# Eleven more product tiles for the first expert steps of a two-layer kernel, and a new order of work

## The chip, the core and the metric

The kernel runs on one core of a Trainium2 chip. A core has five engines with a queue of instructions each: TensorE (PE in the profile) multiplies matrices and writes to eight PSUM banks, VectorE (DVE), ScalarE (ACT) and GpSimd (POOL) do elementwise work, and SyncE (SP) issues the DMA transfers. Each engine takes its own instructions strictly in order; semaphores order the engines against one another. The metric is the device time of one execution in microseconds.

## What is computed

Two transformer-like layers on x of shape (4, 512, 128), all in float32. Cut to what matters:

```python
xn = layernorm(x)
x = x + linear_attention(xn) + mixture(xn)      # layer 1
#   mixture: 64 experts of width 88 and a shared one; 8 experts per token by a grouped top-k
#   rw = route(xn)                               # (tokens, 64), eight non-zero per token
#   out = shared(xn) + sum_e rw[:, e] * ((silu(xn @ Wg[e].T) * (xn @ Wu[e].T)) @ Wd[e].T)
xn = layernorm(x)
x = x + window_attention(xn) + bitlinear_ffn(xn) # layer 2
#   window attention: 8 heads of 16, for each token the 32 nearest of the last 64 by a learned distance
```

## The kernel before

**Expert steps.** The routed and shared experts are stacked and cut into 46 slabs of 128 hidden units (`NF`), the same for each of the four batch rows, so there are 184 expert steps n. In a step TensorE makes the gate part in a bank G and the up part in a bank U, each as three matmuls of 512 columns (high weights by high input, high by low, low by high), ScalarE writes silu(G) into a product tile, VectorE multiplies the tile by U (`products`), and for the 44 routed slabs of each row the tile is multiplied by the spread routing weights `Rb[k]`: even steps on VectorE (`weights`), odd ones on GpSimd (`tiles`). TensorE then adds `WdT @ tile` to bank A (`downs`); a float32 matmul shows as two records. Before a step, ScalarE makes the high part of the weights (`Whi`) and GpSimd or VectorE the low part (`Wlo`).

**The ring.** The product tiles are five, `S[n % RING]`. `silus` therefore waits, before step n writes its tile, until the down matmul of step n-5 is done. With two banks G and two banks U, TensorE itself can run two steps beyond the last tile.

**Where routing weights come from.** Row 0's routing is a long row of small VectorE instructions (letters y): normalise, gate, grouped top-8, weights; then TensorE turns them (`MATMUL bank_X<-cst,xn`, the fourth y of its queue), ScalarE and VectorE make `RW`, and four small matmuls (`bank_X<-RW,sel`, letter s) with a ScalarE copy each give `Rb[0]` to `Rb[3]`. Slabs 0 and 1 need no routing; slab 2 does. So no more than two down matmuls can run before `Rb[0]` exists.

**Other work.** Linear attention of row b (letters a: the matmuls q0, q1, k0, k1, then qn = `bank_X<-cst,PR`, kn = `bank_X<-PR,cst`, sim = `bank_X<-GWk,wqk`, r0, r1 = `bank_X<-wout,z`, m, att) is a chain over four engines: between kn and r0 lie a VectorE clamp, ScalarE logarithm and exponential, four GpSimd passes over `PR` and `z`, and a softmax that goes to and fro. The setup of layer 2's weights (u) is a chain of VectorE instructions with four TensorE steps, wf and wp among them. Layer 2 of row b (h head, d distances, k top-32 by MAX8 and MATCH_REPLACE8 on VectorE, g and t gather, f feed-forward) starts when bank A of the row has been copied to `mo`.

**Order.** The order on each engine is written out by hand as a string of letters in `ORDER` (lines 37 to 72); `weave` takes the next step of the part that each letter names. A letter e on TensorE is half an expert step (G or U), so 368 stand there; m is one down matmul. On ScalarE x is `Whi`, e is silu; on GpSimd l is `Wlo`, m a weighted tile. ScalarE has two function tables to load in turn, one for silu and gelu and one for logarithm and exponential; a load is issued wherever neighbours in the string need different ones (`logarithms`, L1264, and the automatic one, L1259).

Of the kernel before, what the change touches and what calls it, by code (L numbers as in the profile page):

```python
# [15 lines left out]
NF = 46  # L16
# [28 lines left out]
        "eeeeemmeeeehheemmmeeemymmeeemeemahheeemeaehemadedadmeeeadeedatdateemmmeemeeedtemetmdemeameemteeateat"
        "eeaemmestemstfeemfemfetetftemmefmmetfteeeeemfeeeefmsmeemmmeeeetmmtetseeteeeeatmeehmmeemmmteaeeeeeeeh"
        "mhmmeeehhmhmheeehmeeemeeemeemameeehmeeededmdeaedaeemmaetdaeemmdtmeeemeeeeememeeetdatdmeematmteeeamma"
        "teeeetftemeeeemmemfeeetmtemeteemeememeeteftmeeemmteteemmtmtmfhftffthfhhfhhhhfffhfdddfdfdtfttdtddtttt"
# [5 lines left out]
        "gemkaeklemaygyeyemkkyykegleemkkfkgekmkeklekmfgeemeelfgefgemgeemhhhhlyhheyyyyyeyyyyymeehylyyyeyyyeymm"
        "yyeemlheemyeelmhaehhheaoemoolemookkkkkkakokaekoakkgoeemkeakklekamkgkaeemkklemekgemkkakkagkleemkkkgek"
        "fekmgekkkfemkgkkelkefkekkmleefmgemeemglegeeemlgaehhhhemhhgaeemleemhehhelmeemeemlehhheoomeolemooekkkk"
        "akkekoakmkakkeklekgmaooeekamkeelmakkkekgemkegkkkakkaelgmeemkekkklgemefkemgekkkelmkkeegemkkgkeelmgkke"
        "megfhhhhgfhhgfhhhfhhfhooookkfkkokkkkkkkookokkkkggfkkkgkkkkkgkgkkkkkgkgkkgkkkkkkkkggggg",
    "act":
        "xyxxyyxeexcxeecxxeexxexayasxsseeysaexxxeeaexxeeaxauxexeeuxxeuxexeeyxexyexexexexexeexxeexexexexexxeex"  # L60
        "xxeexeexxeyexxsexexeyxmexeesexxxssxexehxeexexyeyhexxexhhxexehxexehxheeehxkekxyenxknknnkaxnxankkngeka"
        "nngexxeenxeaxexexeexxnegxaengaxeexxexexgssyefeexxgxexexeefxexxfegexxfexgsxesmyexexeyhxehxhxeeehxexxe"
# [4 lines left out]
        "lllyyllllllmammaaaamlalalmalmllmlmllmylmyllmmlllmlmllmymlllmlmllmlmllmlmllmlllmllmlmyyllhmolmllmylhm"
        "holmooomoqoaopaqaaalalqllamplpmllmaqlmmlpqlppmqllmlmlmpllqplpmqllmmlplplpymlylmlholmlmllymlmllmmlhlh"
        "olooolaqloooaammalapqalmqampallpmlqlmlpmlqlppmqmlplqmllmqlmplpmllmpllplpmllmlmlholmmllmlmhllholomoom"
        "loaqoaaaalmlopalmllaqmaqllmplpmqqpllmlmlppmqllmllqpmmlppmqmppphohhoooooqoqoqpppqqpppqppqpqpp",  # L70
# [1660 lines left out]
```

## Time and profile before

| | |
|---|---|
| three runs | 785.96, 787.54, 788.20 us; median 787.54 |
| profiled execution | 788.22 us, its span 786.4 us |
| busy, share of the span | PE 90%, DVE 81%, POOL 57%, ACT 53% |
| granted TensorE clock, mean | 0.932 of full |
| chain that ended last | PE 44%, DVE 35%, POOL 7%, ACT 5%, issue 5%, DMA 4% |

The span is the profiled execution from its first to its last instruction; 1.8 us of the execution's own time lie outside it. Busy shares are means over stages that differ: TensorE is nearly full from 16 us to 690 us, VectorE nearly full in some stretches and not in others, and after the last expert step the work is a chain. The chain of waits is followed back from the last instruction, so its shares say who held the end up.

### The profile page before, as it was taken

What the parts mean: (1) busy time and instruction counts of PE and PEld (TensorE: products, weight loads), DVE (VectorE), ACT (ScalarE), POOL (GpSimd) and SP (SyncE); (2) the same over time, 40 slices, a digit from 0 to 9 for tenths busy, and PEclk for the clock granted to TensorE, in tenths of its full rate; (3) what the DMA queues carried; (4) which work ended last, traced back from release to release, by engine and by line L of the source; (5) the groups of instructions that cost most, each with busy time, mean ns of one, the idle gap of its engine ahead of it and who ended that gap; (6) DMA issues with size and microseconds to landing.
All of it is one profiled execution on the core that took longest, in us unless ns stands there. A gap on an engine that the chain in (4) does not pass through costs nothing.

```text
span 786.4 us, 11674 instructions
## 1 busy us (share of the span) xinstructions
PE 704.6 (90%) x3368; PEld 500.7 (64%) x3368; DVE 640.7 (81%) x2562; ACT 419.7 (53%) x757; POOL 451.9 (57%) x535
## 2 busy tenths in 40 slices
PE   3998999999999889999998999999998999978733
PEld 2645666666576666776676677666675776768623
DVE  3877787768999999849799999765799899659974
ACT  3754444566675555455675774456683754465300
POOL 2265366546676864854567856654668768433441
PEclk9979999999997999999998999999999999996555
DMA  9920000000000000000000000001000000010000
GB/s 287 358 68 1 1 0 0 2 1 16 17 1 10 9 15 11 9 15 20 13 1 8 11 12 16 8 7 26 14 2 9 10 15 15 19 31 8 18 23 17
DMA packets 25695, 22.14 MB, mean 28 GB/s; under 512 B 1892, under 2 KB 23424, under 8 KB 25120
## 3 DMA queue, kind: packets, MB, share of 16 engines
q1 hardware_dynamic: 25632, 21.40, 9.1%
q8 instruction: 27, 0.44, 0.2%
q14 instruction: 36, 0.29, 0.1%
HBM read 19.17 MB, written 2.23 MB: 27 GB/s over the span
## 4 chain that ended last, share of the span: by engine, by line
PE 44%; DVE 35%; POOL 7%; ACT 5%; issue 5%; DMA 4%; SPq 0%; DVEq 0%; POOLq 0%; ACTq 0%
PE bank_A L505 11%; PE bank_X L505 11%; PE bank_U L505 10%; PE bank_G L505 9%; DVE Wk L1193 8%; DVE S L790 6%; DVE m L1190 6%; DMA vw<-vscratch 4%; DVE GWk L790 2%; DVE sm L794 1%; POOL wT L1501 1%; POOL Wlo L1501 1%; ACT Ed L1259 1%; DVE wT L790 1%; ACT L1264 1%
## 5 line engine op out<-in xcount | busy, mean ns | idle before, releaser
L505 PE MATMUL bank_A<-S,WdT 128*128 128x512 f32 x368 | 186.8, 612 | 5.9 <-POOL S L1501 4.4
L1501 POOL TENSOR_TENSOR Wlo<-Wgu,Whi 128x256 fp32r<-128x256 f32 x138 | 108.3, 789 | 108.8 <-ACT Whi L1259 108.4
L790 DVE TENSOR_TENSOR S<-S,bank_U 128x512 f32<-128x512 f32 x184 | 123.7, 678 | 56.9 <-PE bank_U L505 36.0
L1259 ACT ACTIVATE S<-bank_G 128x512 f32<-128x512 f32 x184 | 108.2, 594 | 106.7 <-PE bank_G L505 98.0
L1501 POOL TENSOR_TENSOR S<-S,Rb 128x512 f32<-128x512 f32 x88 | 117.8, 1340 | 63.3 <-DVE S L790 59.3
L1259 ACT ACTIVATE Whi<-Wgu 128x256 fp32r<-128x256 f32 x184 | 74.0, 413 | 78.7 <-PE bank_U L505 69.8
L505 PE MATMUL bank_G<-xH,Whi 128*128 128x512 f32 x184 | 96.9, 526 | 5.5 <-POOL Wlo L1501 2.8
L505 PEld LDWEIGHTS bank_A<-S,WdT 128*128 128x128 f32 x368 | 66.7, 193 | 49.9 <-issue 29.2
L505 PE MATMUL bank_U<-xH,Whi 128*128 128x512 f32 x184 | 91.7, 498 | 5.0 <-DVE S L790 4.6
L790 DVE TENSOR_TENSOR S<-S,Rb 128x512 f32<-128x512 f32 x88 | 83.4, 951 | 2.4 <-ACT Rb L1259 0.5
L1193 DVE MATCH_REPLACE8 Wk<-m,Wk 128x79 f32<-128x79 f32 x384 | 81.8, 223 | 0.0
L505 PE MATMUL bank_G<-xL,Whi 128*128 128x512 f32 x184 | 73.5, 400 | 0.0
L505 PE MATMUL bank_U<-xH,Wlo 128*128 128x512 f32 x184 | 73.3, 399 | 0.0
L505 PE MATMUL bank_G<-xH,Wlo 128*128 128x512 f32 x184 | 73.3, 399 | 0.0
L505 PE MATMUL bank_U<-xL,Whi 128*128 128x512 f32 x184 | 73.3, 398 | 0.0
L1501 POOL TENSOR_TENSOR wT<-wT 128x256 f32<-128x256 f32 (+1 forms) x62 | 41.4, 667 | 42.9 <-DVE wT L790 40.5
L1190 DVE MAX8 m<-Wk 128x8 f32<-128x79 f32 x384 | 63.2, 225 | 0.0
L505 PEld LDWEIGHTS bank_G<-xH,Whi 128*128 128x128 f32 x184 | 35.2, 191 | 28.4 <-issue 23.2
L505 PEld LDWEIGHTS bank_U<-xH,Whi 128*128 128x128 f32 x184 | 35.1, 191 | 27.3 <-DVE S L790 12.7
L1259 ACT ACT_TABLE_LOAD x35 | 44.9, 1283 | 1.5 <-PEq L1721 0.7
L505 PEld LDWEIGHTS bank_G<-xL,Whi 128*128 128x128 f32 x184 | 35.4, 193 | 15.5 <-issue 11.4
L505 PEld LDWEIGHTS bank_U<-xL,Whi 128*128 128x128 f32 x184 | 35.2, 191 | 12.6 <-issue 8.1
(233 smaller groups left out, 1440.9 us busy)
## 6 DMA issues: line engine op xcount, KB each, us to landing
vw<-vscratch SPq DMA_DIRECT2D x32, 158.0 KB
Wgu<-in_Wgu SPq DMA_DIRECT2D x2, 2048.0 KB, 15.3
xs<-in_x SPq DMA_DIRECT2D x4, 256.0 KB, 7.0
wqk<-in_w_qkv SPq DMA_DIRECT2D x1, 1024.0 KB, 7.3
Wgu<-in_Wgu SPq DMA_DIRECT2D x1, 1024.0 KB, 9.6
vscratch<-mo SPq DMA_DIRECT2D x4, 256.0 KB
out<-xs SPq DMA_DIRECT2D x3, 256.0 KB, 2.3
Wgu<-in_Wgu SPq DMA_DIRECT2D x1, 512.0 KB, 5.1
```

Of the source, the lines that this page charges most:

```text
L505: return engine.matmul(dst, lhsT, rhs, start=start, stop=stop)
L790: return engine.tensor_tensor(dst, a, b, op)
L794: return engine.tensor_scalar(dst, a, s1, None, op0)
L1190: top[i] = own(engine.max(w8[:, i, 8 * r:8 * r + 8], v[:, i, :]))
L1193: p = engine.match_replace(wk[:, i, :], w8[:, i, 8 * r:8 * r + 8], v[:, i, :], TAKEN)
L1259: return engine.activation(dst, src, f, bias=bias, scale=scale, accum_out=acc)
L1264: engine.preload_act_table_set(LNEXP)
L1501: return engine.tensor_tensor(dst, a, b, op)
```

## The change

Eleven tiles of layer 2, which nothing writes until layer 2 of row 0 begins, take the products of steps 0 to 10. Steps 11 on go round the five tiles `S` as before, shifted. So the first step that must wait for a down matmul is step 16 (for that of step 11), where it was step 5. The helper `early_tile` takes 512 columns of a tile. With that, all five strings of `ORDER` are other strings; no instruction with data is added or taken away, but there are 74 table loads in ScalarE's program where there were 64.

```diff
@@ ORDER, the start of the string of TensorE and of ScalarE; the other strings differ in the same way
-        "yyeeyeeeeemaeeeaemaeeeeeeyaesasmsmsmaeeaeeeemmmmmmeeemeeamueamaueeeeuemmeeeaumeeeeyeeemmyeeemymmmeem"
+        "yyeeyyeeemeemeeeaeeaeeaeeeeeeeeeeeaeyaeseesmammsasmmmmmuemmmeemauaeeeeaemmueammumeeeeyeeymeeeeeemy"
-        "xyxxyyxeexcxeecxxeexxexayasxsseeysaexxxeeaexxeeaxauxexeeuxxeuxexeeyxexyexexexexexeexxeexexexexexxeex"
+        "yxxxyyexexexecexxceexxeexexexxeaeaxxyexsesxyassaeexaaxexeuxexuuxeeyxxeeeyexxxexexxeeexxeexxexexyexey"
...
+        early = [mo, yT, ksq, hf, hg, wT[0], wT[1], kp, mk2, Ed[0], Ed[1]]
+
+        def early_tile(t):
+            return (t[:, :, :].rearrange("p a w -> p (a w)") if len(t.shape) == 3 else t)[:, 0:T]
+
+        tiles_of = [early_tile(t) for t in early] + [t[:, :] for t in S]
+
+        def product_tile(n):
+
+            return tiles_of[n] if n < len(tiles_of) else S[(n - len(early)) % RING][:, :]
+
+        def tile_free(n):
+
+            return n - RING + 1 if n >= len(tiles_of) else 0
...
-                    if n >= RING:
-                        sc_.wait_ge("down", n - RING + 1)
-                    emptied(act(S[n % RING][:, :], t[:, :], ACT.Silu), "g", n)
+                    if tile_free(n):
+                        sc_.wait_ge("down", tile_free(n))
+                    emptied(act(product_tile(n), t[:, :], ACT.Silu), "g", n)
...
-                    mm(T_["A"][:, :], WdT[:, m % NF, :], S[m % RING][:, :], m % NF == 0, m % NF == NF - 1).then_inc(
+                    mm(T_["A"][:, :], WdT[:, m % NF, :], product_tile(m), m % NF == 0, m % NF == NF - 1).then_inc(
```

`products`, `weights` and `tiles` take `product_tile(n)` in the same way.

**TensorE around the turned routing weights of row 0** (`bank_X<-cst,xn` from L514, which is L529 in the changed file). Before:

```order
58 L505 MATMUL bank_G<-xL,Whi 128x512
59 L505 MATMUL bank_G<-xH,Wlo 128x512
60 L514 MATMUL bank_X<-cst,xn 128x128 x4
61 L505 MATMUL bank_X<-wqk,Gs 128x512
62 L505 MATMUL bank_U<-xH,Whi 128x512
63 L505 MATMUL bank_U<-xL,Whi 128x512
64 L505 MATMUL bank_U<-xH,Wlo 128x512
65 L505 MATMUL bank_X<-RW,sel 128x512
66 L505 MATMUL bank_X<-cst,PR 128x1 x8
67 L505 MATMUL bank_X<-RW,sel 128x512
68 L505 MATMUL bank_A<-S,WdT 128x512
69 L505 MATMUL bank_X<-RW,sel 128x512
```

The changed kernel at the same place:

```order
87 L520 MATMUL bank_X<-wqk,Gs 128x512
88 L520 MATMUL bank_G<-xH,Whi 128x512
89 L520 MATMUL bank_G<-xL,Whi 128x512
90 L520 MATMUL bank_G<-xH,Wlo 128x512
91 L529 MATMUL bank_X<-cst,xn 128x128 x4
92 L520 MATMUL bank_X<-cst,PR 128x1 x8
93 L520 MATMUL bank_U<-xH,Whi 128x512
94 L520 MATMUL bank_U<-xL,Whi 128x512
95 L520 MATMUL bank_U<-xH,Wlo 128x512
```

The turn stood behind 17 half expert steps and two down matmuls; it now stands behind 27 half steps and the same two down matmuls.

**GpSimd from the same place to the end of the key norms of row 0** (`PR`, `z`: the attention chain; `<-...,Rb`: weighted products). Before:

```order
10 L1501 TENSOR_TENSOR Wlo<-Wgu,Whi 128x256 x6
11 L1501 TENSOR_TENSOR S<-S,Rb 128x512
12 L1501 TENSOR_TENSOR PR<-GWk,wqk 128x1024
13 L1501 TENSOR_TENSOR S<-S,Rb 128x512 x2
14 L1501 TENSOR_TENSOR PR<-PR 128x512
15 L1501 TENSOR_TENSOR PR<-PR,z 128x512
16 L1562 TENSOR_SCALAR PR<-PR 128x512
17 L1501 TENSOR_TENSOR z<-PR 128x512
```

The changed kernel:

```order
10 L1516 TENSOR_TENSOR Wlo<-Wgu,Whi 128x256 x9
11 L1516 TENSOR_TENSOR PR<-GWk,wqk 128x1024
12 L1516 TENSOR_TENSOR Wlo<-Wgu,Whi 128x256
13 L1516 TENSOR_TENSOR hf<-hf,Rb 128x512
14 L1516 TENSOR_TENSOR Wlo<-Wgu,Whi 128x256
15 L1516 TENSOR_TENSOR wT<-wT,Rb 128x512
16 L1516 TENSOR_TENSOR kp<-kp,Rb 128x512
17 L1516 TENSOR_TENSOR Ed<-Ed,Rb 128x512
18 L1516 TENSOR_TENSOR S<-S,Rb 128x512
19 L1516 TENSOR_TENSOR PR<-PR 128x512
20 L1516 TENSOR_TENSOR PR<-PR,z 128x512
21 L1577 TENSOR_SCALAR PR<-PR 128x512
```

Between the wide `PR<-GWk,wqk` and the first `PR<-PR` stood two weighted products; five weighted products and two `Wlo` stand there now.

**ScalarE at the head of layer 2 for row 2**, expert steps 150 to 153. In the kernel before:

```order
457 L1259 ACT_TABLE_LOAD
458 L1259 ACTIVATE hb<-bank_X,b 64x1
459 L1259 ACTIVATE Whi<-Wgu 128x256
460 L1259 ACT_TABLE_LOAD
461 L1259 ACTIVATE S<-bank_G 128x512
```

In the changed kernel, where the attention of row 3 (`rq`, `PR`, `z`) stands among it:

```order
459 L1279 ACT_TABLE_LOAD
460 L1274 ACTIVATE rq<-rq 128x8 x2
461 L1274 ACTIVATE PR<-z 128x512
462 L1274 ACTIVATE PR<-PR 128x512
463 L1274 ACT_TABLE_LOAD
464 L1274 ACTIVATE S<-bank_G 128x512
465 L1274 ACTIVATE Whi<-Wgu 128x256
466 L1274 ACTIVATE mo<-bank_X 128x512
467 L1274 ACT_TABLE_LOAD
468 L1274 ACTIVATE hb<-bank_X,b 64x1
469 L1279 ACT_TABLE_LOAD
470 L1274 ACTIVATE z<-z 128x512
```

The attention of row 3 came between expert steps 158 and 168 of VectorE's string; it comes between 145 and 163 now.

## Rows read from the trace of the kernel before

**Rows 1.** Busy time by stretch: us, then busy us (instructions) of each engine, PEclk.

```profile
16.29:36.40 20.11, 19.98 (x69) 13.94 (x69) 18.04 (x62) 13.48 (x22) 5.38 (x10) 1.00 1.04 367
36.40:63.70 27.30, 25.24 (x102) 12.33 (x102) 19.19 (x43) 12.52 (x24) 17.15 (x14) 0.81 0.30 79
...
480.00:560.00 80.00, 78.98 (x321) 52.62 (x321) 57.01 (x175) 41.24 (x79) 42.30 (x54) 1.00 0.06 15
560.00:690.00 130.00, 121.22 (x675) 89.65 (x674) 114.41 (x527) 74.07 (x130) 89.75 (x103) 0.99 0.04 12
```

**Rows 2.** Timeline of TensorE, 35 to 64 us: start, us, instruction, releaser.

```profile
35.51 0.40 PE L505 MATMUL bank_G<-xH,Whi 128*128 128x512 f32 x1
...
37.37 0.66 PE L514 MATMUL bank_X<-cst,xn 128*128 128x128 f32 x4 [0.99 <-DVE xn L795]
...
39.51 0.50 PE L505 MATMUL bank_X<-RW,sel 32*128 32x512 f32 x1
39.94 2.01 PE L505 MATMUL bank_X<-cst,PR 128*128 128x1 f32 x16
```

**Rows 3.** Timeline of TensorE, 82 to 93 us, at full clock.

```profile
82.31 0.39 PE L505 MATMUL bank_G<-xH,Whi 128*128 128x512 f32 x1
...
83.00 0.40 PE L505 MATMUL bank_U<-xH,Whi 128*128 128x512 f32 x1
...
92.97 0.40 PE L505 MATMUL bank_G<-xH,Whi 128*128 128x512 f32 x1
```

**Rows 4.** The chain of waits, three pieces: start, us, what.

```profile
7.98 1.28 ACT L1264
...
343.63 1.72 PE bank_A L505 x4
...
608.93 1.28 ACT L1264
```

**Rows 5.** Timeline of VectorE: `RW`, weighted products, attention of row 3.

```profile
38.69 0.75 DVE L798 SCALAR_TENSOR_TENSOR RW<-RW,cst,bank_X 128x512 fp32r<-128x512 f32 x1 [0.79 <-ACT RW L1259]
40.68 5.11 DVE L790 TENSOR_TENSOR S<-S,Rb 128x512 f32<-128x512 f32 x3 [0.45 <-ACT Rb L1259]
62.39 0.68 DVE L790 TENSOR_TENSOR S<-S,Rb 128x512 f32<-128x512 f32 x1
...
586.13 0.68 DVE L794 TENSOR_SCALAR z<-bank_X 128x512 f32<-128x512 f32 x1
...
611.07 0.67 DVE L1038 TENSOR_REDUCE rq<-z 128x8 f32<-128x512 f32 x1
```

**Rows 6.** Timeline of GpSimd, row 0's attention chain and its neighbours.

```profile
42.45 2.79 POOL L1501 TENSOR_TENSOR PR<-GWk,wqk 128x1024 f32<-128x1024 f32 x1
...
54.17 1.20 POOL L1501 TENSOR_TENSOR PR<-PR 128x512 f32<-128x512 f32 x1 [4.36 <-ACT PR L1259]
...
60.01 0.74 POOL L1501 TENSOR_TENSOR Wlo<-Wgu,Whi 128x256 fp32r<-128x256 f32 x1
```

**Rows 7.** Timeline of TensorE, where the first r of the attention starts.

```profile
68.77 1.09 PE L505 MATMUL bank_X<-wout,z 64*64 64x128 f32 x16
```

**Rows 8.** Costliest groups: line engine op, count | busy us, mean ns | idle before.

```profile
L1501 POOL TENSOR_TENSOR S<-S,Rb 128x512 f32<-128x512 f32 x88 | 117.8, 1340 | 63.3 <-DVE S L790 59.3
L1193 DVE MATCH_REPLACE8 Wk<-m,Wk 128x79 f32<-128x79 f32 x384 | 81.8, 223 | 0.0
L1190 DVE MAX8 m<-Wk 128x8 f32<-128x79 f32 x384 | 63.2, 225 | 0.0
```

**Rows 9.** Timeline of ScalarE, 7 to 10 us.

```profile
7.55 0.42 ACT L1259 ACTIVATE Whi<-Wgu 128x256 fp32r<-128x256 f32 x1 [5.54 <-DMA WdT<-in_WdT]
7.98 1.28 ACT L1264 ACT_TABLE_LOAD   x1
9.28 0.45 ACT L1259 ACTIVATE lnv<-lnv 128x8 f32<-128x8 f32 x2
```

**Rows 10.** Who waited for whom, 0 to 100 us: one row of ScalarE's tile waits.

```profile
ACT S L1259 <- PE bank_A L505: 2.0, 3, 1.0
```

More of the change, by code:

```diff
@@ L45 @@
[L45 to L48, printed above, removed]
+        "yyeeyeeemeemeeeaeeaeeaeeeeeeeeeeeeaeyaeseesmammsasmmmmmuemmmeemauaeeeeaememmueammumeeeeyeeymeeeeeemy"
@@ new lines @@
+        "mmeeeemeeemeeeemmmeeemmeeemeyeeemmeemeeesmmseeseemsmeeeeememememememeeeeeymeyemmyheeeeeeemmmemeeeeee"
+        "heehhmmeheeeemmmeehehmemmeheemeymeeeemhmemeeedeeadeemedeadmdamemateetademeeaeeeaemmmdteemeeetmdmemee"
+        "emmatetmaeeaeteeemetatemesmeesememfeetetmfteeemmfteetmemfeetfeeemmeethmtfmfteeeeefeetseeesemmeymmeet"
+        "ymmmyheehhemeehhemhehmeeemeememeeeeemmeheeymeeeaeeeaeeadadadmadadememmtmmtdemeememeetdeeeemmaetemaed"
+        "eaemtetmaeeeesmmeemmteestefeeftemmeeetmefteeefetefemmfteetemfmmmefeeesetmeseetatatheteememamaeeeaeeh"
@@ L54 @@
[L54 to L58, printed above, removed]
@@ new lines @@
+        "ylyyeyeyeyyyyylemeyyymeyyymeyyeyymleeyeymyyemyyelemeemleemeelmeeeemlyyhehehehmyylyhyyeeyyheyyyymyeyy"
+        "lmhyeemyyyyeemelmhehheemhemylehooemeoemlaoeokkakkkkkkkokkaeeoeglkekaokakmmemekakkkeamkleeamgegkkklem"
+        "ekakgemekkaekgklmyeemykegekkfkklgemkkkgkeyfekmelkyygeemhhfghheeelmfemgelemeghyhyyyyyyyyyemhyeyyhyyyh"
+        "yelmyeemyhyeelymehemheoeylemaemoaooaokakakolekokkkkkaemegaemokkkelkemakkkeekkekgmkelmagkeakkeemklekg"
+        "mekkekgmefkklgemekkeefmkkgkfkegmkkkklefeelemgeagaemhghehhhhemlaeemaghaaeahaemhleehmehhelmoeoemooeemk"
@@ new lines @@
+        "klokkkkkkekookkgemoekkkemlkegeakkmkelkgkemekkemeklkakeegmemekkgeklmekkemgeklekmgkfkeemkeklemkegkemke"
+        "kgghfhhhgfhhgfhhhhfhhfooofkkkokkkkokkookkkfkogkgkkkkkkkkgkgkgkkkkkkkkkkkggkgkkkkkggggg",
+    "act":
+        "yxxxyyexexexecexxceexxeexexexxeaeaxxyexsesxyassaeexaaxexeuxexuuxeeyxxeeeyexxxexexxeeexxeexxexexyexey"
+        "xeesxxsesxexexexexexexxeesxyemxyexeexxxheexxeexhxehhexxheeexxexhexexhexeyhxekxkxeeknxkennkxnennkkaxe"
+        "gnaexkxexeaxnexnegxexenaxeexnagxaexneexxegxesexxsefexgxexegfexxeyxeemxfxgegfexexxexsxseexeyehyxhxhhe"
+        "xhexxeexheexxxeheexhxekkyxeexxxankaknnnxkaeknnkenegxekeanxxxeneexxgeanxaexneneexgxxsexesefgxxexexefe"
+        "gxxexfexgexfexxexsemseegxgxxeahaexexhxehaexhhaexxeehehxxexhexkeknexknxenxxakknexanenngxkkenkneegxxxe"
+        "neexxexennexxgexxeexegxfeexexxexgexxeexefgxxeeeegmgfhfhhhhfhhfhkfnnkknnnnkknnknnfgnnkkgnngnnggggg",
@@ L66 @@
     "pool":
[L67 to L70, printed above, removed]
+        "lllyylllllllllalmlmmmmaaaaaamalmmlllmylylmmllmllmmllmlymlllmmlllmmllmllmlyyllmmllllmlmholmlymlmlhlml"
@@ L71 @@
+        "homllomolmolooqlamolpmlaqqaaallamlaqmappmlllmqpmllplpmlqmllpqmpplmlqllpmlmllpplmyymllholmllmhlmymllh"
+        "olllooaoaammaaqmoolalmapqolmlaqlmllmpqpmllmlqpmllpplqmmllmlqplppqmllmlpllmpplamlhoaaaaamalalmhmllhol"
+        "molomllolqoomqopmllqmplplmqlmlmllqmlpmlpplmqllmlplmqlmpmpmqppphohhooooqooqopqppqpqppqqpppqpp",
 }
@@ L814, in products @@
                 for n in range(total):
-                    s = S[n % RING]
+                    s = product_tile(n)
                     yield
```

26 lines of the change are left out of this document (9 added, 17 removed).

## The prediction

> **What bounds the kernel now.** I read first the busy time by stretch [rows 1]; its columns after the length are PE, weight loads, DVE, ACT, POOL, the granted clock, DMA share and GB/s. From 16.29 to 36.40 us TensorE is busy 19.98 of 20.11 us and VectorE 18.04: both are near full, since row 0's routing and the first expert steps go on together. From 36.40 to 63.70 TensorE looks busy (25.24 of 27.30) but at a mean clock of 0.81. Later VectorE alternates: 57.0 of 80 us from 480 to 560, where row 2's experts are finished, and 114.4 of 130 from 560 to 690, where the top-k work of layer 2 lies beside the experts.
>
> The timeline of TensorE then shows what "busy" hides [rows 2]. Half step 16 starts at 35.51. The turn of the routing weights waits 0.99 us for VectorE and starts at 37.37. The spread that follows takes 0.43 us to its successor (39.51 to 39.94), and then comes qn, sixteen records of one column, 2.0 us; behind it the clock drops to 1.2 GHz until about 52 us. TensorE has nothing better to do there: with five tiles, and only steps 0 and 1 free of routing, it stands at most two steps beyond tile 6. The wait itself is hardly visible: ScalarE waited for a tile 2.0 us in three pieces [rows 10], because the old order never let it come to a longer one.
>
> How much is lost, by counting. A half expert step takes 0.69 us at full clock (82.31 to 83.00, [rows 3]), a down matmul 0.86 (1.72 for two, [rows 4]). From half step 16 at 35.51 to half step 40 at 92.97 are 57.5 us. In them stand 24 half steps (16.6 us), 15 downs (12.9 us), and other work of about 16.9 us at full clock, an estimate from the timeline: turn 0.5, four spreads 1.7, k1 0.9, qn 1.9, kn 1.1, sim 1.15, r0 and r1 2.2 ([rows 7] has one), m 1.95, att 1.05, the layer 2 setup 4.45. That is 46.4, so 11.1 us of the stretch are lost to low clock and to waiting.
>
> **The change part by part.** *Start.* ScalarE's string now begins with the logarithm of the lengths instead of `Whi`. Before, `Whi` waited for a transfer until 7.55 and the table load began at 7.98 [rows 9]; the lengths are ready at about 7.2, so the routing chain, and with it TensorE's first expert step, comes 0.7 us earlier.
>
> *Filling the hole.* Ten more half steps stand ahead of the turn. They cost TensorE 6.9 us there, and VectorE six more products and a `Wlo`, some 4.5 us in its full stretch; so `RW`, which is made at 38.69 now [rows 5], comes later. From 34.8 (35.51 less 0.7) eleven half steps and k1 bring TensorE to the turn at 43.3. VectorE is ready for it by then (its 4.5 us more on 37.4, less 0.7, is 41.2), so nobody waits there, and after it TensorE has steps for which no routing is wanted. If it never waits until half step 40, it gains the 11.1 us and the 0.7: 11.8.
>
> *What is late next.* The chain of linear attention. In GpSimd's queue five weighted products and two `Wlo` now stand between the wide `PR` product and the first `PR<-PR`. Turn at 43.3 plus 0.5, qn 1.9, wide product 2.79 [rows 6], two `Wlo` at 0.74 [rows 6], five weighted products at 1.34 [rows 8]: GpSimd comes to the chain at 56.7, not at 54.17. From there to r0 it took 14.6 us (54.17 to 68.77, [rows 6, 7]), of which one weighted product and one `Wlo` (2.1 us) no longer stand in between: r0 at 69.2. TensorE has before r0, counted from 34.8, 17 half steps (11.7), 12 downs (10.3), k1, qn, kn and sim (5.0), spreads, turn and the first setup step (2.5): it is there at 64.3 and waits 4.9 us, with the setup's wf, r1 and four half steps queued behind. So of 11.8 the front keeps 6.9. Bounds: 11.8 if the wait is hidden; about 0 if GpSimd's five products are as slow as beside VectorE's and the clock drops behind qn as it does now (three downs at 2.0 instead of 0.86 and their neighbours, 5 us).
>
> The row on that: VectorE took 5.11 us for three weighted products while GpSimd worked, and 0.68 for one alone [rows 5]. The Trainium skill, "GPSIMD Engine Reference", section 1, Specifications, says that GpSimd shares its SBUF interfaces with VectorE and contends with VectorE instructions that have two SBUF inputs; by that rule, and this trace agrees, bunching eleven weighted products on both engines speaks against the change. With a stretched duration in place of the mean, r0 and the total would come some 2 us later.
>
> *Ten more table loads.* There are 64 pieces of 1.28 us now, and on the chain that ended last stand ten of them, the first at 7.98, the last at 608.93 [rows 4]. If the ten new ones lie on the chain as often, 10 x 10/64 x 1.28 = 2.0 us. Bounds: 0 and 12.8. The activation behind a load starts at 9.28, 0.02 us after its end [rows 9]. The Trainium skill, "ScalarE: Activation LUTs", section What ACT_TABLE_LOAD costs, gives 1.28 us for the load and 1.38 for a drain, 2.66 together; the load agrees, the drain is not seen here. By the page this term would be 4.2 us.
>
> *Attention of row 3.* It moves from VectorE's steps 158 to 168 to its steps 145 to 163, out of the full stretch and partly into the one with slack [rows 1]. Its four passes of 512 columns on VectorE at 0.68 ([rows 5]: first at 586.13, last at 611.07) are 2.7 us, with the small ones about 5.4. I take 2.7 as gained; bounds 0 and 5.4. What pays is the head of layer 2 for row 2, among which it now stands, in part by the table loads above.
>
> *Tail.* Behind the last expert step the strings are the same but for one more round of top-k and one more turn. A round is four MAX8 and four MATCH_REPLACE8 at 0.22 [rows 8], 1.8 us; it stands where VectorE also waits for `mo`, so I take half, 0.9 (bounds 0 and 1.8).
>
> *Between.* From 93 to 690 us all strings differ, but the milestones stand within a few steps of their old places relative to the experts, and all work is the same. Its stalls I take as unchanged, with 5 us to either side.
>
> Sum: -6.9 + 2.0 - 2.7 + 0.9 = -6.7 us. On the profiled execution's 788.2 that is 781.5; the median is 0.7 below that execution, so 780.8.
>
> **The rivals.** *More of it is kept.* If the wait for r0 is hidden and the attention of row 3 gives its full 5.4: -11.8 - 5.4 + 2.0 + 0.9 = -14.3, 773. For it: the chain up to 84 us runs over the setup's VectorE steps, which are also earlier now. Against it: GpSimd's queue, counted above.
>
> *The gain in front is given back.* Stretched products and a clock that falls behind qn leave about nothing in front; table loads and row 3's attention cancel: 788. For it: the clock fell behind qn in this very place. Against it: half steps follow qn now, not a spread and a tile that isn't ready, and no idle time stands ahead of it.
>
> *Table loads at the head of row 2.* Seven of the ten new loads are in expert steps 150 to 169 (17 instead of 10), between `ln`, `hb`, `met` and the distances, which feed the top-k that fills VectorE afterwards. If all ten are on the path, 12.8 instead of 2.0: -6.9 - 2.7 + 0.9 + 12.8 = +4.1, 791.6. It turns to slower from about seven loads on the path (8.7/1.28). For it: ten loads are on the chain now, several of them at such heads. Against it: at 480 to 560 us VectorE has 23 us to spare.
>
> *The tiles do nothing.* If the old order had lost its time not to the ring but to VectorE's routing chain alone, more tiles would only add work ahead of it. Against it: the loss is after 37.4, when the routing is done. This ends like the second rival and shares its chance.
>
> **How the numbers follow.** Forecast, 776 to 785: 0.46. More kept, under 776: 0.19. Given back, 785 to 790: 0.18. Slower by table loads or by another stall of the new order: 0.17. A measurement here tells 0.3% (2.4 us) from no change. So faster 0.65, same 0.18, slower 0.17. The range 771 to 791 leaves 0.05 below and 0.14 above; the forecast's own is 776 to 785.
>
> **What would show it.** Right: in the new timeline TensorE reaches the turn at 42 to 45 us without a wait; the clock between 36 and 64 us stays near 1; half step 40 with 20 downs done stands at about 88 to 90 us (before, with three downs less, 92.97); r0 starts at 68 to 71 with several us of idle before it, and GpSimd's z or PR ahead of it in the chain; 74 table loads. `mo` of row 3 is copied 5 to 8 us earlier than now. Wrong: a clock of 0.5 behind qn again; an idle TensorE between 43 and 60; a top-k of row 2 that starts no earlier than before.

## The result, and the profile after

| | before | after |
|---|---|---|
| median of the runs | 787.87 us (4) | 806.62 us (4; 803.84 to 808.82) |
| span of the profiled execution | 786.4 us | 806.6 us |
| granted TensorE clock, mean | 0.932 | 0.925 |

The ratio is 1.0238, its 95% interval [1.0196, 1.028]: the changed kernel is 18.8 us slower, where 6.7 us faster was forecast. It lies above the range too. That it is slower is clear; whether by more than 2% isn't, since the interval begins at 1.0196.

The stretches of [rows 1] in the changed kernel, and one more, in the same columns:

```profile
16.29:36.40 20.11, 20.08 (x74) 14.84 (x75) 17.11 (x57) 14.26 (x23) 5.03 (x9) 1.00 1.04 367
36.40:63.70 27.30, 22.81 (x107) 13.00 (x106) 25.12 (x49) 12.89 (x27) 18.15 (x16) 0.89 0.30 80
400.00:440.00 40.00, 36.39 (x197) 25.61 (x196) 28.77 (x85) 26.04 (x45) 23.70 (x26) 0.87 0.01 2
480.00:560.00 80.00, 78.73 (x399) 54.87 (x397) 65.19 (x277) 42.21 (x81) 52.96 (x66) 1.00 0.05 13
560.00:690.00 130.00, 121.07 (x587) 85.61 (x587) 116.31 (x513) 78.85 (x133) 83.86 (x94) 0.99 0.05 13
```

From 36.4 to 63.7 us VectorE (the third number pair) went from 19.2 to 25.1 us of busy time, and TensorE was busy for 22.8 us instead of 25.2. Right behind it, from 64 to 93 us, TensorE is as busy as before, but at a granted clock of 0.87 (the third number from the end) where the kernel before had 1.00; the changed kernel stands first:

```profile
64.00:93.00 29.00, 27.38 (x122) 18.08 (x121) 23.47 (x42) 8.15 (x14) 10.94 (x10) 0.87 0.00 1
64.00:93.00 29.00, 27.30 (x142) 18.52 (x141) 22.18 (x46) 12.14 (x22) 11.15 (x11) 1.00 0.00 1
```

From 400 to 440 VectorE had 28.8 us of work; in the kernel before it had 37.9:

```profile
400.00:440.00 40.00, 36.72 (x229) 29.32 (x229) 37.92 (x179) 27.87 (x46) 29.50 (x29) 0.91 0.02 6
```

**The front.** TensorE's timeline, where [rows 2] and [rows 7] stood:

```profile
43.22 0.60 PE L529 MATMUL bank_X<-cst,xn 128*128 128x128 f32 x4
43.66 1.84 PE L520 MATMUL bank_X<-cst,PR 128*128 128x1 f32 x16
...
51.24 2.07 PE L520 MATMUL bank_A<-ksq,WdT 128*128 128x512 f32 x2 [2.50 <-DVE ksq L805]
...
58.53 0.69 PE L520 MATMUL bank_X<-GWk,wqk 128*64 128x64 f32 x16 [1.33 <-DVE z L809]
72.99 1.09 PE L520 MATMUL bank_X<-wout,z 64*64 64x128 f32 x16
```

The turn comes at 43.22 us with no wait. Then TensorE waits 2.50 us for the first weighted product (`ksq` is one of the new product tiles), and `r0` starts at 72.99. Why, VectorE and GpSimd show between 50 and 60 us, where [rows 5, 6] had their products:

```profile
51.11 1.75 DVE L805 TENSOR_TENSOR hg<-hg,Rb 128x512 f32<-128x512 f32 x1
52.77 1.75 DVE L805 TENSOR_TENSOR wT<-wT,Rb 128x512 f32<-128x512 f32 x1
54.45 1.75 DVE L805 TENSOR_TENSOR mk<-mk,Rb 128x512 f32<-128x512 f32 x1
56.12 1.75 DVE L805 TENSOR_TENSOR Ed<-Ed,Rb 128x512 f32<-128x512 f32 x1
57.80 0.68 DVE L809 TENSOR_SCALAR z<-bank_X 128x512 f32<-128x512 f32 x1
...
59.08 0.69 DVE L805 TENSOR_TENSOR S<-S,Rb 128x512 f32<-128x512 f32 x1
```

```profile
50.60 1.70 POOL L1516 TENSOR_TENSOR wT<-wT,Rb 128x512 f32<-128x512 f32 x1
52.27 1.71 POOL L1516 TENSOR_TENSOR kp<-kp,Rb 128x512 f32<-128x512 f32 x1
53.94 1.71 POOL L1516 TENSOR_TENSOR Ed<-Ed,Rb 128x512 f32<-128x512 f32 x1
55.62 1.71 POOL L1516 TENSOR_TENSOR S<-S,Rb 128x512 f32<-128x512 f32 x1
59.88 1.06 POOL L1516 TENSOR_TENSOR PR<-PR 128x512 f32<-128x512 f32 x1 [2.55 <-ACT PR L1274]
```

A product on each engine at the same time takes 1.75 us on VectorE and 1.7 on GpSimd; VectorE's next one, with GpSimd waiting, takes 0.69. The clamp of `kn` (`z<-bank_X`, 0.68 us of work, its matmuls issued from 53.24) stands behind four stretched products, and GpSimd then waits 2.55 us for what ScalarE makes of it.

**Row 1's distances.** TensorE after the metric of row 1 (`nm`) in the changed kernel, then VectorE, then both in the kernel before:

```profile
404.61 1.05 PE L520 MATMUL bank_X<-ksq,nm 128*72 128x512 f32 x2 [1.92 <-DVE nm L809]
...
417.96 0.34 PE L520 MATMUL bank_X<-mk,rr 128*128 128x79 f32 x2
```

```profile
419.91 0.68 DVE L805 TENSOR_TENSOR La<-Pk,cst 8x512 f32<-8x512 f32 x1 [3.26 <-PE bank_X L520]
422.56 0.69 DVE L805 TENSOR_TENSOR rr<-kp,cst 128x512 f32<-128x512 f32 x1 [1.97 <-PE bank_X L520]
...
427.21 0.37 DVE L1205 MAX8 m<-Ed 128x8 f32<-128x79 f32 x2
```

```profile
395.74 1.05 PE L505 MATMUL bank_X<-ksq,nm 128*72 128x512 f32 x2 [0.99 <-DVE nm L794]
...
399.04 0.34 PE L505 MATMUL bank_X<-mk,rr 128*128 128x79 f32 x2
```

```profile
407.65 0.53 DVE L1190 MAX8 m<-Ed 128x8 f32<-128x79 f32 x3 [0.81 <-ACT Ed L1259]
```

Between the two matmuls the new order has ten half steps, one down, row 3's turn and three matmuls `wqk,Gs` (two records each); the old one has one half step, one down and one `wqk,Gs`. The first distance comes 13.4 us after the metric instead of 3.3, and top-k, the work that fills VectorE, starts 19.6 us later. Of these 19.6 us, 8.9 lie ahead of the metric (404.61 against 395.74).

**The tail.** SyncE's queue and the last wait of TensorE for it:

```profile
710.01 59.44 SPq L424 DMA_DIRECT2D vw<-vscratch  x6
769.55 8.29 SPq L424 DMA_DIRECT2D out<-xs  x1
777.89 8.72 SPq L424 DMA_DIRECT2D vw<-vscratch  x2
```

```profile
781.67 2.04 PE L520 MATMUL bank_U<-wT,vw 79*128 79x128 f32 x8 [4.78 <-DMA vw<-vscratch]
790.39 2.04 PE L520 MATMUL bank_U<-wT,vw 79*128 79x128 f32 x8 [1.38 <-DMA vw<-vscratch]
798.89 2.05 PE L520 MATMUL bank_U<-wT,vw 79*128 79x128 f32 x8 [5.61 <-DMA vw<-vscratch]
```

A store of the output holds SyncE 8.29 us ahead of the last two loads. In all TensorE waited 14.7 us for these loads in four pieces, before 8.5 in two. SyncE's string differs here: in the old order four of row 3's eight loads stand ahead of its first store, in the new one six. No run isolates what that costs.

How far each kernel had come (milestones from the timelines, us; `mo` is the copy that ends a row's experts):

| | mo, rows 0 to 3 | first MAX8 of layer 2, rows 0 to 3 |
|---|---|---|
| before | 160.7, 345.4, 520.4, 676.5 | 227.7, 407.7, 575.4, 706.6 |
| after | 169.7, 345.4, 529.9, 693.4 | 239.8, 427.2, 596.9, 723.3 |

### The profile page after: what moved, and what is told of

It is laid out like the page before. It is cut to its first block, busy times and chain, and to the rows that moved or that the text cites. A ratio compares the mean times of both kernels' runs of the same rounds, so it can differ in the third digit from the quotient of the medians.

```text
span 806.6 us, 11677 instructions
## 1 busy us (share of the span) xinstructions
PE 712.0 (88%) x3368; PEld 501.7 (62%) x3368; DVE 648.4 (80%) x2562; ACT 430.3 (53%) x767; POOL 451.2 (56%) x535
## 4 chain that ended last, share of the span: by engine, by line
DVE 41%; PE 40%; DMA 6%; issue 5%; ACT 4%; POOL 4%; SPq 0%; DVEq 0%; POOLq 0%; ACTq 0%
PE bank_X L520 12%; PE bank_G L520 10%; PE bank_U L520 9%; DVE S L805 9%; DVE Wk L1208 8%; PE bank_A L520 7%; DMA vw<-vscratch 5%; DVE m L1205 5%; DVE GWk L805 2%; DVE wT L805 2%; DVE Wlo L805 1%; ACT L1279 1%; DVE sm L809 1%; PE bank_X L775 1%; PE bank_X L529 1%
## 5 line engine op out<-in xcount | busy, mean ns | idle before, releaser
L520 PE MATMUL bank_A<-S,WdT 128*128 128x512 f32 x346 | 177.3, 617 | 7.2 <-DVE S L805 6.6
L805 DVE TENSOR_TENSOR S<-S,bank_U 128x512 f32<-128x512 f32 x173 | 116.2, 680 | 50.0 <-PE bank_U L520 26.3
L1516 POOL TENSOR_TENSOR S<-S,Rb 128x512 f32<-128x512 f32 x84 | 114.0, 1359 | 73.1 <-DVE S L805 72.6
L1274 ACT ACTIVATE S<-bank_G 128x512 f32<-128x512 f32 x173 | 101.4, 594 | 94.0 <-PE bank_G L520 77.9
L520 PE MATMUL bank_U<-xH,Whi 128*128 128x512 f32 x184 | 95.7, 520 | 2.9 <-DVE S L805 2.8
L520 PEld LDWEIGHTS bank_A<-S,WdT 128*128 128x128 f32 x346 | 63.6, 196 | 46.3 <-issue 25.9
L805 DVE TENSOR_TENSOR S<-S,Rb 128x512 f32<-128x512 f32 x83 | 75.7, 914 | 1.7
```

What stands on the lines that cost most here:

```text
L805: return engine.tensor_tensor(dst, a, b, op)
L1274: return engine.activation(dst, src, f, bias=bias, scale=scale, accum_out=acc)
L1516: return engine.tensor_tensor(dst, a, b, op)
```

## The experiments

Gaps are in us, medians against medians of the kernel before on the same chip. A kernel that is old in one stretch and new in another is joined at an expert half step of TensorE, on all engines at once: each engine ends its first part where it stands when TensorE comes to that half step by a rough count of durations, and the rest of its letters follow in the other order. Half step 48 lies at about 105 us, 128 at 210, 192 at 345, 240 at 445, 288 at 530. Each expectation names its theories by letters; a letter can mean another theory in the next one.

**The tiles alone**: the changed kernel with all the strings of the old order. In the diffs of orders the first letters that differ stand.

```diff
 "pe":
-    "yyeeyeeemeemeeeaeeaeeaeeeeeeee
+    "yyeeyeeeeemaeeeaemaeeeeeeyaesa
...
```

> The eleven borrowed product tiles, but every engine in the order of the kernel before. Theory O (the new order costs the time, the tiles as such are free): 786 to 790 us, within 0.3% of before. Theory T (the tiles cost: a product in a borrowed tile is slower to write or read, or holds something up): 800 or more. If the ring's own waits mattered in the old order, up to 2 us faster, since ScalarE waited 2.0 us for a tile in the first 100 us.

Measured: 788.78 us, 1.0006 [0.9987, 1.0025]. In the old order the tiles cost nothing and give nothing; the whole loss comes with the order.

**The new order up to a half step, the old behind it**, and the reverse for 48. At the joint of the first:

```diff
 "pe":
...
-    eeymeeeeeemymmeeeemeeemeeeemmm
+    eeymeeymmeemeeeemmeeemeeemeeee
...
```

> The tiles and the new order up to half expert step 48 (about 105 us, where TensorE of both kernels stands at the same point within 1.2 us, 2 downs fewer in the new one), then the remaining steps in the order of before. Theory F (the new front is neutral or a small gain, the loss is in the rest): 784 to 790. Theory D (the front hands over a debt on VectorE and GpSimd that shows only later, as mo 9 us late): 795 to 807.

> The tiles and the order of before up to half expert step 48, then the remaining steps in the new order. Theory F (the loss is in the rest): 802 to 808. Theory D (the debt of the new front): 786 to 793. If both halves cost, in between, and the two losses add up to 19.

> The tiles and the new order up to half expert step 128 (about 216 us, into the head of layer 2 of row 0), then the order of before. In the trace of the changed kernel the first top-k starts at 239.8 instead of 227.7 us, so 12 of the 20 us are there by then. If this loss is carried to the end: 796 to 802. If the old order of the rest absorbs it: 787 to 791.

> The tiles and the new order up to half step 192 (345 us, where row 1's mo is copied at 345.4 us in before and in the changed kernel), then the order of before. Cut at 128 gave 1.0100 of before, the whole new order 1.024. Theory H (the loss that is left is made after this point, where the new order puts row 1's head of layer 2 behind twelve half steps and a routing: mo to kp 32.7 us against 15.2): 1.008 to 1.013, 794 to 798. Theory K (it is made while row 0's top-k work is woven among row 1's experts, VectorE busy 99.5 of 120 us against 114.5): 1.016 or more, 801 or more.

> The same with the cut at half step 240 (453 us in the changed kernel, row 1's first top-k lies behind it at 427). Theory H: row 1's head is now in the new order, so 1.018 to 1.026, 802 to 808, clearly above the cut at 192. Theory K: as the cut at 192, within 0.3%.

| new up to half step | us | ratio, 95% interval | gap |
|---|---|---|---|
| 48 | 791.69 | 1.0031 [1.0003, 1.0059] | 3.6 |
| 128 | 795.89 | 1.0100 [1.0074, 1.0126] | 7.8 |
| 192 | 801.71 | 1.0163 [1.0128, 1.0198] | 13.3 |
| 240 | 808.50 | 1.0245 [1.0214, 1.0277] | 20.1 |
| all (the changed kernel) | 806.62 | 1.0238 [1.0196, 1.028] | 18.8 |
| old to 48, then new | 803.85 | 1.0196 [1.0172, 1.0221] | 15.8 |

Against the expectations: new to 48 lies just above theory F's range, old to 48 inside it, and new to 128 at the lower edge of a carried loss. New to 192 is theory K's number and new to 240 is H's, which speaks against either as the only cause.

The front is no gain and a small loss (the old front takes only 3 us off), and each further stretch to 240 costs something. There is no single bad place. In the kernel new up to 128 the delay is carried: `mo` of rows 0 to 3 is copied 7, 7, 7 and 9 us later than before.

**No table loads**: functions that share a table, in both orders. It leaves out SiLU in the experts and GELU in the metric (Relu in their place), and with them all but one or two of the loads.

```diff
-    emptied(act(S[n % RING][:, :], t[:, :], ACT.Silu), "g", n)
+    emptied(act(S[n % RING][:, :], t[:, :], ACT.Relu), "g", n)
...
-    act(hb[:, :], ps("met", b)[0:64, 0:1], ACT.Gelu, bias=b1[:, 0:1]).then_inc(sems("hb"), 1)
+    act(hb[:, :], ps("met", b)[0:64, 0:1], ACT.Relu, bias=b1[:, 0:1]).then_inc(sems("hb"), 1)
```

> The kernel before with Relu in place of Silu and Gelu, so that ScalarE has 2 table loads instead of 64; the values are others, every other instruction is the same. If ten of 64 loads lie on the path, as the chain of waits shows, 10 x 1.28 = 13 us less: about 775. If the loads are hidden: 786 to 789.

> The changed kernel with Relu in place of Silu and Gelu, 1 table load instead of 74. Theory L (the ten more loads, at the heads of layer 2, make the loss): it falls to within 3 us of the kernel before without loads. Theory O (the places of the other instructions make it): it stays 14 to 19 us above that kernel. My rival on record priced the loads at up to 12.8 us.

Measured: the old order 780.99 us (0.9914 [0.9882, 0.9945]), the new one 799.85 (1.0129 [1.0086, 1.0171]). Either gives back about 7 us and the gap between them stays 18.9. The old order's gain lies between the 13 us of loads on the path and the nothing of hidden ones; of the second pair, theory O was right. Ten loads more are not what costs: the gaps are known to some 4 us each, so the 2.0 of the prediction isn't excluded, but 12.8 is.

**The attention chain first**: new to 48, with row 0's chain ahead of the bunched products.

```diff
 "pe":
...
-    aeseesmammsasmmmmmuemmmeemauae
+    aeseesammmsasmmuemmmmmmeemauae
...
 "dve":
...
-    yyyyammmmmaamyyau
+    yyyyaaammmmmmyyau
...
 "pool":
...
-    lalmlmmmmaaaaaamalmml
+    lalmlaaaamaammmalmmml
```

> The changed order up to half step 48 and the old one behind it (that gave 1.003 of the kernel before), with one edit in its front: on TensorE, VectorE and GpSimd the chain of linear attention of row 0 now goes ahead of most of the bunched weighted products (VectorE has its kn clamp three letters earlier, GpSimd the whole powers of PR with three products behind them, TensorE its sim three downs earlier and r0 four). Theory Q (the front gave nothing because the attention chain stood behind the products in two queues): r0 at 65 to 68 us instead of 73, and the kernel ends below the kernel before: 0.992 to 0.999, 782 to 787 us. Rival W (the front is bound by VectorE's work as such, and the order in its queue matters little): r0 at 70 or later, 1.001 to 1.005, 789 to 792 us.

Measured: 802.70 us, 1.0181 [1.0154, 1.0208]: 11 us worse than the same kernel without the edit. GpSimd, VectorE and TensorE in it:

```profile
53.13 1.04 POOL L1516 TENSOR_TENSOR PR<-PR 128x512 f32<-128x512 f32 x1 [2.71 <-ACT PR L1274]
...
71.82 1.11 POOL L1516 TENSOR_TENSOR z<-z,rq 128x512 f32<-128x512 f32 x1 [1.92 <-DVE rq L1054]
```

```profile
65.03 3.73 DVE L810 TENSOR_SCALAR GWk<-rr,bsc 128x128 f32<-128x128 f32 x4
68.79 1.39 DVE L810 TENSOR_SCALAR GWk<-GWk 128x512 f32<-128x512 f32 x1
...
70.82 0.68 DVE L1053 TENSOR_REDUCE rq<-z 128x8 f32<-128x512 f32 x1
```

```profile
79.35 2.07 PE L520 MATMUL bank_A<-S,WdT 128*128 128x512 f32 x2 [3.33 <-POOL S L1516]
81.36 0.91 PE L520 MATMUL bank_X<-wout,z 64*64 64x128 f32 x6
```

In the kernel without the edit (new to 48) GpSimd starts the chain at 56.6 and its last `z` at 69.4, and `r0` starts at 70.8. With the edit the chain starts 3.5 us earlier and ends 2.4 us later. The next thing in VectorE's queue, the setup of layer 2, is stretched: the first line of VectorE's above took 1.68 us in the kernel without the edit. TensorE reaches `r0` 10.6 us later, behind downs whose products GpSimd had put back (it waits 3.33 us for one of them). Theory Q fell as it was put, and W's number was passed as well: moving the chain is not enough. That the three queues have to fit is how the trace reads; no run shows a front in which they do.

**GpSimd with one input**: its weighted products and `Wlo` in forms that read one tile, in both orders. It leaves out the routing weights of odd steps and the low part of GpSimd's split weights.

```diff
-    tt(Wlo[w][:, :], Wgu[:, n % NF, :], Whi[w][:, :].bitcast(F), ALU.subtract).then_inc(sems("wlo_p"), 1)
+    engine.tensor_scalar(Wlo[w][:, :], Wgu[:, n % NF, :], 1.0, 1.0, ALU.mult, ALU.mult).then_inc(sems("wlo_p"), 1)
...
-    tt(s, s, Rb[k][:, :], ALU.mult).then_inc(sems("tw_p"), 1)
+    po.wait_ge(*own(engine.tensor_scalar(s, s, 1.0, 1.0, ALU.mult, ALU.mult)))
+    engine.tensor_scalar(s, s, 1.0, 1.0, ALU.mult, ALU.mult).then_inc(sems("tw_p"), 1)
```

> The kernel before with GpSimd's weighted products and its Wlo in forms with one input: each weighted product of an odd step is two tensor_scalar by 1.0 instead of one tensor_tensor with the routing weights, each Wlo of GpSimd one tensor_scalar instead of the subtraction. It leaves out the routing weights of the odd steps and the low part of half the split weights. It is the base of the next kernel. Theory C (VectorE and GpSimd disturb each other when both read two tiles, and that costs in either order): somewhat faster than before, 0.985 to 0.995, and VectorE's weighted products beside GpSimd at about 0.7 us each. Theory H (the new order delays the heads of layer 2): the same within 1% here, nothing more can be told from this one.

> The changed kernel with the same two edits as the kernel next to it. Theory C: the new order is slow because it bunches products with two inputs on both engines; with one-input forms on GpSimd VectorE's four products after 51 us take 0.7 instead of 1.75 us each, r0 comes at 67 to 69 us and the gap between the orders shrinks from 19 us to less than 8. Theory H (the order itself delays the heads of layer 2 from half step 48 on): the front gets its 4 to 5 us back, but the gap stays at 12 to 18 us.

Measured: 768.24 us in the old order (0.9745 [0.9719, 0.9772]), 778.05 in the new one (0.9876 [0.9843, 0.9908]). The gap is halved, to 9.8 us, and `r0` comes at 70.4. Neither theory had that: C wanted less than 8, H 12 or more; 9.8 is known to about 3 us, so it doesn't part them. The old order gained more than C gave it. The edit changes more than the contention: GpSimd's own busy time falls from 451.9 to 407.7 us in the old order, so the gain can't be put down to contention alone. VectorE's four products in the new order now, where C gave 0.7:

```profile
47.96 1.09 DVE L805 TENSOR_TENSOR hg<-hg,Rb 128x512 f32<-128x512 f32 x1
48.97 0.88 DVE L805 TENSOR_TENSOR wT<-wT,Rb 128x512 f32<-128x512 f32 x1
49.77 1.09 DVE L805 TENSOR_TENSOR mk<-mk,Rb 128x512 f32<-128x512 f32 x1
50.79 1.09 DVE L805 TENSOR_TENSOR Ed<-Ed,Rb 128x512 f32<-128x512 f32 x1
```

**The same for the first 24 expert steps alone**, in the new order.

```diff
-    tt(s, s, Rb[k][:, :], ALU.mult).then_inc(sems("tw_p"), 1)
+    if n < 24:
+        po.wait_ge(*own(engine.tensor_scalar(s, s, 1.0, 1.0, ALU.mult, ALU.mult)))
+        engine.tensor_scalar(s, s, 1.0, 1.0, ALU.mult, ALU.mult).then_inc(sems("tw_p"), 1)
+    else:
+        tt(s, s, Rb[k][:, :], ALU.mult).then_inc(sems("tw_p"), 1)
...
```

> The changed kernel with GpSimd's weighted products and Wlo in forms with one input (each product two tensor_scalar by 1.0, each Wlo one) for the first 24 expert steps alone; it leaves out the routing weights and the low parts there. Theory C (half of the gap is the products bunched on VectorE and GpSimd in front, which the trace shows as 7 us more VectorE time before 93 us, carried to the end): 796 to 801 us, 1.011 to 1.017, with r0 at 67 to 70 us. Rival L (what the one-input forms gave, 28 us in the changed kernel and 21 in the one before, came from all rows alike, and the front's part is lost again later): 803 to 807 us, 1.020 to 1.025.

Measured: 800.84 us, 1.0146 [1.0096, 1.0195], `r0` at 69.2. That is theory C's number: 12.0 us above the kernel before, where the changed kernel is 18.8 above. But the old order wasn't given this edit, so 12.0 isn't a gap between two orders under the same edit, and how much of the 6.8 us the old order would gain too stays open. The edit on all steps moved `r0` in the old order as well, by 3.3 us (68.8 to 65.5) against 2.6 in the new one; these are single traces, and those with the unchanged old front have `r0` from 67.0 to 70.0.

**The old order between half steps 192 and 240**, new on both sides.

```diff
 "pe":
...
-    tfmfteeeeefeetseeesemmeymmeety
+    tfmfteftsstyeeyemmeyeemhmehhee
...
```

> The changed kernel with one piece of the old order: between half steps 192 and 240, where the head of layer 2 for row 1 is, all engines take their steps in the order of the kernel before; ahead of it and behind it they follow the new order. New order to 192 and old behind it gave 801.7 us, new order to 240 and old behind it 808.5, all new 806.6. Theory H (what this piece loses is row 1's head, which stands behind the routing of row 3 on VectorE, and the loss is carried to the end): 798 to 802 us, ratio 1.013 to 1.018, with row 1's first top-k at about 418 instead of 427 us. Rival D (the loss is a drift that settles at some level whichever piece is old, since a later piece catches up with what an earlier one lost): 804 to 808 us, 1.020 to 1.025.

Measured: 810.64 us, 1.0277 [1.0245, 1.0309]. H fell, and D as well: it is no better than the new order, rather worse. Row 1's first top-k did come at 420 us and not 427, and the copy of `mo` of row 2 stayed at 530.1: what the stretch won was lost again before the next milestone. That the order behind it has its own places for the next steps is a reading of this, not shown.

**A cheap top-k**: both orders, with all rounds but the last on 8 of 79 columns (most of the choice of neighbours is left out).

```diff
-    v = src if r == 0 else wk
+    v, c = src, (79 if r == rounds - 1 else 8)
...
-    top[i] = own(engine.max(w8[:, i, 8 * r:8 * r + 8], v[:, i, :]))
+    top[i] = own(engine.max(w8[:, i, 8 * r:8 * r + 8], v[:, i, 0:8]))
...
-    p = engine.match_replace(wk[:, i, :], w8[:, i, 8 * r:8 * r + 8], v[:, i, :], TAKEN)
+    p = engine.match_replace(wk[:, i, 0:c], w8[:, i, 8 * r:8 * r + 8], v[:, i, 0:c], TAKEN)
```

> The kernel before with a cheap top-k: all rounds but the last read and write 8 of the 79 columns, and each looks at the same 8. It leaves out most of the choice of neighbours and takes some tens of us of work from VectorE. Base of the next kernel. Both theories expect it faster than before by 20 to 60 us (0.93 to 0.975).

> The changed kernel with the same cheap top-k. Theory V (the new order loses from step 48 on because top-k comes later and then falls into stretches in which TensorE needs VectorE): with less top-k on VectorE the gap between the orders, 19 us now, shrinks to less than 9. Theory T (TensorE and VectorE wait for each other at single steps of the experts and of the heads in the new order, whatever the top-k weighs): the gap stays at 14 to 22 us.

Measured: 768.19 us (0.9731 [0.9674, 0.9787]) and 785.17 (0.9944 [0.9921, 0.9968]), a gap of 17.0, where the edit took 61 us of busy time off VectorE in the old order and 63 in the new one. Theory V fell: the weight of top-k is not what the new order loses by. The gap is in theory T's range; that single waits make it is not shown by that.

**Where behind 345 us**: the old order to 192 or to 288 and the new behind it, and the new between 192 and 288 alone. At the joint at half step 192, old behind it (-) and new (+):

```diff
 "pe":
...
-    tesemsemmtyeeehyemmmmeyeemhmehhe
+    tesemsemmtyehmmeeeeeeeeeemmemmee
...
```

> The old order up to half step 192 (about 345 us, where all kernels so far have done the same number of expert steps and of MAX8), and the new order behind it; tiles as in the changed kernel. Additive theory A (a delay is made in a piece and carried to the end; new order to 192 cost 13 us): 19 less 13, so 793 to 797 us, 1.006 to 1.012. Rival B (at 345 us the orders are level, so the loss is made in the stretch behind it, by the order there): 800 to 807 us, 1.016 to 1.025.

> The old order with one piece of the new one, from half step 192 (about 345 us) to 288 (about 530 us): the head of layer 2 for row 1, its distances and most of its top-k, beside the experts of row 2. Tiles as in the changed kernel. Theory M (the loss behind 345 us is made there: the new order gives TensorE seven half steps between the metric and the first distances of row 1, and VectorE's top-k starts 12 us later): 798 to 804 us, 1.012 to 1.020. Rival E (it is made later, at the heads of rows 2 and 3 and in the tail): 789 to 794 us, 1.000 to 1.007.

> The old order up to half step 288 (about 530 us), the new one behind it; tiles as in the changed kernel. Theory M (loss between 192 and 288): 790 to 795 us, of which 3 us are the longer tail of the new order, 1.002 to 1.009. Rival E (loss made later): 799 to 804 us, 1.013 to 1.020.

| new where | us | ratio, 95% interval | gap |
|---|---|---|---|
| 192 to the end | 802.26 | 1.0165 [1.0115, 1.0215] | 13.5 |
| 192 to 288 | 793.90 | 1.0066 [1.0039, 1.0093] | 5.7 |
| 288 to the end | 797.05 | 1.0113 [1.0083, 1.0144] | 8.9 |

The first was B's number, not A's. The second was E's, the third lay between the two theories: the loss is in both pieces, more of it in the later one. Their 5.7 and 8.9 make 14.6, against 13.5 for both at once, within the intervals. (The seven half steps of M's text are ten in the rows above.) Row 1's distances follow the piece that holds them, here with the new piece and then with the old:

```profile
392.85 1.05 PE L520 MATMUL bank_X<-ksq,nm 128*72 128x512 f32 x2 [0.58 <-DVE nm L809]
...
404.60 0.34 PE L520 MATMUL bank_X<-mk,rr 128*128 128x79 f32 x2
```

```profile
392.98 1.05 PE L520 MATMUL bank_X<-ksq,nm 128*72 128x512 f32 x2 [0.96 <-DVE nm L809]
...
396.28 0.34 PE L520 MATMUL bank_X<-mk,rr 128*128 128x79 f32 x2
```

So the long way from the metric to the distances comes with the new piece, but its price isn't seen in this trace: the profiled execution of the kernel with the new piece took 788.5 us, the shortest of its ten and as long as that of the kernel before. Row 1's first MAX8 comes at 413.8 there instead of 407.7, row 2's at 576.2 instead of 575.4.

In the last kernel (new from 288) row 2's first MAX8 comes at 585.7 us instead of 575.4, though `mo` was 2 us early. VectorE and the stretches of TensorE there:

```profile
571.16 3.97 DVE L805 TENSOR_TENSOR rr<-kp,cst 128x512 f32<-128x512 f32 x1
...
584.40 0.69 DVE L805 TENSOR_TENSOR S<-S,bank_U 128x512 f32<-128x512 f32 x1 [3.75 <-PE bank_U L520]
```

```profile
571.00:576.00 5.00, 3.52 (x27) 3.06 (x25) 4.96 (x4) 2.80 (x6) 4.39 (x5) 0.97 0.00 0
576.00:580.00 4.00, 4.00 (x16) 3.69 (x16) 1.77 (x4) 0.54 (x2) 1.43 (x1) 0.50 0.00 0
```

One `rr` product of 0.67 us takes 3.97 while GpSimd does four instructions; TensorE is idle for 1.5 of 5 us; behind that the granted clock is 0.50, its lower level, for four; and VectorE waits 3.75 us for TensorE in its turn. From the copy of row 3's `mo` (681.8) to the end this kernel takes 113.1 us, the kernel before 109.9: by these two traces 3.2 of the 8.9 are the tail.

## Why the prediction was wrong

*Between.* "Its stalls I take as unchanged, with 5 us to either side": this is the step that failed most, the term "Between", put at 0. With the old front the new order from half step 48 on costs 15.8 us, of which the tail is some 3.2. Behind half step 192 alone it costs 13.5; in pieces, 5.7 up to half step 288 and 8.9 from there on, the tail among it. The milestones did stand within a few steps of their old places, as the prediction says, and it meant nothing: ten half steps between a metric and its distances are "a few steps", and VectorE runs dry there (it waits 3.26 and 1.97 us for TensorE in the rows above). The diff and the list of instructions show this place, and the prediction looked at the heads for table loads only. That this one place makes the 5.7 us wasn't isolated.

*What is late next.* The right wait was named, the chain of linear attention behind the products in GpSimd's queue, and mis-sized: five products at the mean of 1.34 us took 1.7, VectorE's took 1.75 instead of 0.68, and the clamp of `kn` in VectorE's queue wasn't looked at. `r0` came at 73.0, not 69.2. The Trainium skill, "GPSIMD Engine Reference", section 1, Specifications, speaks of this contention, the trace agrees (1.75 against 0.68 us), and the prediction priced it at 2 us and left it out of the sum. Half step 40 with 20 downs stood at 96.6 us, not at 88 to 90.

*Filling the hole.* TensorE was at the turn at 43.2 (43.3 forecast) without a wait, and the clock held behind `qn`. But "a clock near 1" was right only there: from 36 to 64 us it was 0.89, from 64 to 93 it was 0.87, and the loss had moved behind the products, with TensorE idle 2.50 us ahead of the first of their downs. Of the 6.9 us nothing was kept: new to half step 48 is 3.6 slower, not faster. With one-input forms in the first 24 steps the changed kernel is about 6.8 us faster; how much of that the old order would gain too was not measured, so the part of contention in the gap is not shown. Rival "given back" had the mechanism, at 788, but not its sign.

*Ten more table loads.* Taken at 2.0 us, with 12.8 as the rival. All but one or two of the loads cost about 7 us in either order, 0.1 us each, and the ten more can't be told from nothing. That rival named the right side and the wrong cause; the 0.17 for slower also covered "another stall of the new order", which named none.

*Attention of row 3.* Taken as 2.7 gained. It stands in the stretch from 288 on, which lost 8.9; a gain of that size isn't seen, and was not measured by itself.

*Tail.* 0.9 forecast, some 3.2 in the traces. The prediction took the strings there as the same but for a round of top-k and a turn; SyncE's isn't, and TensorE's waits for its loads are 6.2 us longer. That this makes the 3.2 is read from the traces, not isolated.

*Start.* The load of the first table began at 7.58 instead of 7.98 [rows 9]: 0.4 us, with 0.7 forecast. TensorE's first expert step, which was to come 0.7 us earlier with it, came no earlier in this trace (16.32, before 16.29).

```profile
7.58 1.28 ACT L1279 ACT_TABLE_LOAD   x1 [7.58 <-DVE lnv L809]
```

*The tiles do nothing* was put as a rival and shared its chance with another. For the tiles alone it is right, to within 0.3%.

The account: 13.5 us are lost behind half step 192 (in pieces, 5.7 from 192 to 288 and 8.9 behind it), and the new order ahead of 192 adds 5.3 to that. What stays open is that new to 192 with the old order behind it costs 13.3, as much as the new order behind 192 alone. The two make 26.8 and not 18.8, so the pieces are not independent: some 8 us are lost only where one order follows the other. So the runs show where the order costs, and not which waits make it up. For the piece behind 288 that is told from one place in one trace, not by an experiment.

## What to carry to other kernels

Where engines work through fixed queues, a new order is not its best stretch: go through every place where one engine's work feeds another's full stretch (here each metric and its first distances) and count what now stands between. Price work on VectorE and GpSimd by what it takes when both work, once it is bunched. And measure more room alone before its order: here the tiles were free, and the whole 19 us came with the order.

## What the runs showed of the hardware

- VectorE and GpSimd disturb each other much. A 128x512 product took 0.68 to 0.69 us on VectorE alone, 0.88 to 1.09 beside GpSimd's one-input form and 1.75 beside its two-input one; GpSimd's took 1.25 alone and 1.7 together. A single `rr` product was seen at 3.97. One-input forms on GpSimd cut VectorE's busy time of the whole kernel from 640.7 to 607.6 us, GpSimd's own from 451.9 to 407.7, and the time by 20.7, more than the 18.8 of the whole change:

```profile
L790 DVE TENSOR_TENSOR S<-S,Rb 128x512 f32<-128x512 f32 x88 | 83.4, 951 | 2.4 <-ACT Rb L1259 0.5
```

```profile
L790 DVE TENSOR_TENSOR S<-S,Rb 128x512 f32<-128x512 f32 x88 | 68.7, 783 | 2.5 <-ACT Rb L1259 0.6
```

(the same group of VectorE in the kernel before, and with one-input forms on GpSimd: 951 and 783 ns).

- The kernel before ran 7 us faster without 62 of its 64 table loads of 1.28 us, so most of their time was hidden.
